# Expert dispatch in a four-stage attention and expert kernel: 64 row scatters into a slot table replaced by 79 row gathers from a token table

## The chip, the cores and the metric

One Trainium2 chip, one core. The metric is the device time of one execution in microseconds (us); the kernel before was run three times. PE is TensorE, ACT is ScalarE, DVE is VectorE, POOL is GpSimd, SP is SyncE.

## What is computed

The input is 16 batches of 128 tokens with 256 channels. Four gated layers follow one another; the change touches only the last, a causal attention followed by a mixture of 16 experts:

```
x2 = rmsnorm(hid, ln2_w).reshape(-1, h)
logits = x2 @ gate_w.T
probs = jax.nn.softmax(logits, axis=-1)
top_w, top_i = jax.lax.top_k(probs, TOPK)                      # TOPK = 4 of E = 16
top_w = top_w / jnp.sum(top_w, axis=-1, keepdims=True)
wfull = jnp.sum(jax.nn.one_hot(top_i, E) * top_w[..., None], axis=1)
gu = jnp.einsum('th,eih->tei', x2, w1)                         # I = 176
act = jax.nn.silu(gu[..., :I]) * gu[..., I:]
routed = jnp.einsum('te,teh->th', wfull, jnp.einsum('tei,ehi->teh', act, w2))
shared = jax.nn.silu(sg) * su @ sh_down_w.T                    # hidden size 352
return hid + (routed + shared).reshape(b, s, h)
```

There are 2048 tokens, so 8192 pairs of token and expert. The kernel sorts them by expert into 79 tiles of 128 slots; a tile belongs to one expert, and slots that are left over in an expert's last tile are empty.

## The kernel before

The last layer ends in two blocks. The first, `sort_and_share` (tiles named e_), normalises the tokens, scores them against the 16 experts, picks four for each, works out the slot of each pair, and computes the shared expert for all tokens. The second, `routed_experts` (tiles named t_), loops over the 79 tiles. A block begins when all engines have ended the one before it.

**sort_and_share.** DVE computes the routing in a chain of small operations, each waiting for its predecessor (`chained`). Its last result is `idx` (L2599), for every token the numbers of its four slots. POOL then issues 64 indirect DMAs (L2342), one for each batch and each of the four choices: each writes 128 rows of 288 floats (the normalised token, 16 expert weights, 16 copies of the token's number) from `rows` to the slots of the DRAM table `slot_rows`, with at most three in flight. The table had been filled with blank rows early in the kernel by one DMA of SP (L787), so that empty slots hold weight zero and a destination in a part of the result that is thrown away. Beside the scatters the shared expert runs in 12 units (4 groups of tokens by 3 tiles of hidden columns): PE `gates_and_values(t)` then `down(t-2)`, ACT `gates(t)` (L2437) then `round_hid(t-1)` (L2443), DVE `hidden(t)` (L2496), `rest_hid(t-1)` (L2501), after each group `add_group` (L2508), and in units 5 to 7 the `tables` that tell the loop which expert each tile has. All four engines work through their lists in order.

**Expert weights.** Each expert's 128x704 weights are loaded into one of 5 buffers (`mw_raw`) and split into a high part by ACT (L2208) and a low part by DVE (L2214). Experts 0 to 4 are split on ACT ahead of the shared expert and on DVE in units 0 to 4; experts 5 to 15 are split once the shared expert is done, because their place in the tile `w_all` holds the shared expert's operands until then.

**routed_experts.** For tile t SP loads 128 slot rows (L2671, six buffers), PE turns them (L2745), ACT and DVE split them into two parts (L2724, L2828), PE multiplies by the gate and value weights (L2764 to L2766), ACT applies silu (L2709), DVE multiplies by the value and the weight (L2822), PE turns the hidden tile (L2773) and multiplies by the second weight (L2783), ACT copies the result to `ysb` (L2714, four buffers), and POOL scatters its 128 rows with an adding indirect DMA into the DRAM tensor `slot_results` (L2700). DVE takes the weight and the destination of each slot out of the slot row with three operations (L2802, L2810, L2815), three tiles ahead; the last of them, `place`, also waits for a scatter some tiles back. POOL issues scatter t only when scatter t-2 has landed. Every 16 tiles PE loads the experts of the next 16 tiles into registers. When all scatters have landed, the two planes of results are loaded and added to x.

Of the kernel before, what the change touches and what calls it, by code (L numbers as in the profile page):

```python
# [7 lines left out]
F32 = mybir.dt.float32  # L8
# [666 lines left out]
def bit_linear_ffn(nc, res, gate_w, val_w, out_w, bias, bias_part, out_b, gate, blank_rows, work):  # L675
# [7 lines left out]
    with ExitStack() as stack:  # L683
# [84 lines left out]
        with nc.Block() as block:  # L768

            @block.sync  # L770
            def _(sp):
# [15 lines left out]
                sp.dma_start(slots.rearrange("(u r) n -> u r n", r=Y_BUFS * P),  # L787
                             fill.unsqueeze(0).broadcast_to([TABLE // Y_BUFS, Y_BUFS * P, ROW])).then_inc(filled, 16)
# [1385 lines left out]
META = 2 * EXPERTS  # L2174
ROW = DIM + META
# [3 lines left out]
EARLY = 5  # L2179
# [9 lines left out]
class ExpertWeights:  # L2189

    def __init__(self, nc, stack, w, w2):
# [6 lines left out]
        self.pick = s.sb("pick", [P, TABLE, EXPERTS], BF16)  # L2198
        self.ld_d = s.sem("ld_d")
# [3 lines left out]
    def load(self, sp, e):  # L2203
        sp.dma_start(self.raw[:, e % RAW_BUFS, :], self.w[e]).then_inc(self.ld_e[e % RAW_BUFS], 16)

# [12 lines left out]
def sort_and_share(nc, x_sb, ident, first, big, ln2, gate_w, gu_w, down_w, consts, gate, slots, filled):  # L2218


    PAD = EXPERTS + 4
    PAIRS = BATCHES // 2
    UNITS_S = GROUPS * SH_TILES
    toks = BATCHES * TOKENS
    spare = [EARLY * 2 * W_COLS]

# [4 lines left out]
    xTh, xTl = (borrow(KT * toks).rearrange("p (k t) -> p k t", k=KT) for _ in range(2))  # L2231
    hid_h, hid_l = (borrow(2 * GT).rearrange("p (a t) -> p a t", a=2) for _ in range(2))
    gu_hf, gu_lf = (borrow(2 * KT * SHARED_HID) for _ in range(2))
    d_hf, d_lf = (borrow(SH_TILES * DIM)[0:SH_ROWS, :] for _ in range(2))
    gu_h, gu_l = (a.rearrange("p (n k c) -> p n k c", n=2, k=KT) for a in (gu_hf, gu_lf))
    d_h, d_l = (a.rearrange("p (j c) -> p j c", j=SH_TILES) for a in (d_hf, d_lf))
    with ExitStack() as stack:
        s = Scope(nc, stack, "e")
        cons = s.sb("cons", [P, P + BATCHES])
        steps = s.sb("steps", [P, EXPERTS * EXPERTS + TABLE])  # L2240
# [3 lines left out]
        raw_gu = s.sb("raw_gu", [P, 2 * KT * SHARED_HID])  # L2244
# [6 lines left out]
        rows = s.sb("rows", [P, BATCHES, ROW])  # L2251
        gw = s.sb("gw", [P, KT, 2, EXPERTS], F32R)
        logits = s.sb("logits", [P, BATCHES, EXPERTS])
# [17 lines left out]
        idx = s.sb("idx", [P, BATCHES, TOPK], mybir.dt.int32)  # L2271
        passed = s.sb("passed", [P, TABLE, EXPERTS + 1], BF16)
        owner = s.sb("owner", [1, TABLE])
        silu = s.sb("silu", [P, 2, GT])
        hid = s.sb("hid", [P, 2, GT])
# [6 lines left out]
        n_ps = l_ps[:, 0, 0, :]  # L2282
        ld_n, ld_g, ld_c, ld_t, ld_s = s.sem("ld_n"), s.sem("ld_g"), s.sem("ld_c"), s.sem("ld_t"), s.sem("ld_s")
# [6 lines left out]
        token_set, c_psum, n_psum = s.sem("token_set"), s.sem("c_psum"), s.sem("n_psum")  # L2290
        idx_ready, meta_ready, sh_hi, sh_lo = s.sem("idx_ready"), s.sem("meta_ready"), s.sem("sh_hi"), s.sem("sh_lo")
# [3 lines left out]
        sent_rows = [s.sem(f"sent_rows{k}") for k in range(IN_FLIGHT)]  # L2295
# [4 lines left out]
        with nc.Block() as block:  # L2300

            @block.sync
            def _(sp):
# [9 lines left out]
                sp.dma_start(first.down[:, :], first.w2).then_inc(first.ld_d, 16)  # L2313
                for n in range(RAW_BUFS, EXPERTS):
                    sp.wait_ge(first.w_lo, n - RAW_BUFS + 1)
                    first.load(sp, n)

            @block.gpsimd
            def _(pool):
# [9 lines left out]
                pool.wait_ge(ld_c, 32)  # L2329
                pool.tensor_copy(rows[:, :, DIM + EXPERTS:ROW],  # L2330
                                 cons[:, P:P + BATCHES].unsqueeze(2).broadcast_to([P, BATCHES, EXPERTS]))\
                    .then_inc(token_set, 1)

                pool.wait_ge(filled, 32)
                pool.wait_ge(token_set, 1)
                pool.wait_ge(idx_ready, 1)
                pool.wait_ge(meta_ready, 1)
                for b in range(BATCHES):
                    for k in range(TOPK):
                        n = TOPK * b + k  # L2340
                        after(pool, sent_rows[n % IN_FLIGHT], 16 * (n // IN_FLIGHT))
                        pool.indirect_dma_start(slots[:, :], bass.IndirectOffsetOnAxis(idx[:, b, k:k + 1], 0),  # L2342
                                                rows[:, b, :], None).then_inc(sent_rows[n % IN_FLIGHT], 16)
                for k in range(IN_FLIGHT):
                    pool.wait_ge(sent_rows[k], 16 * len(range(k, BATCHES * TOPK, IN_FLIGHT)))

            @block.tensor
            def _(pe):
# [8 lines left out]
                def score(m):  # L2357
# [3 lines left out]
                    for b in range(2 * m, 2 * m + 2):  # L2361
                        tok = slice(P * b, P * b + P)
                        for k in range(KT):
                            pe.matmul(l_ps[:, b, :, :], xTh[:, k, tok], gw[:, k, :, :], start=(k == 0), stop=False)
                            mm = pe.matmul(l_ps[:, b, :, :], xTl[:, k, tok], gw[:, k, :, :], start=False,
                                           stop=(k == KT - 1))
# [18 lines left out]

                def gates_and_values(t):
                    (g_, j), p = divmod(t, SH_TILES), t % 2
                    r, c, tok = slice(0, width(j)), slice(SH_ROWS * j, SH_ROWS * j + width(j)), slice(GT * g_, GT * g_ + GT)
                    if t == 0:
                        pe.wait_ge(sh_lo, 2)  # L2390
                    for n, ps, free, done in ((0, g_ps, silu_ready, g_psum), (1, u_ps, hid_ready, u_psum)):
                        after(pe, free, t - 1)
                        for kt in range(KT):
                            h, l = gu_h[:, n, kt, c], gu_l[:, n, kt, c]
                            pe.matmul(ps[p][r, :], h, xTh[:, kt, tok], start=(kt == 0), stop=False)
                            pe.matmul(ps[p][r, :], h, xTl[:, kt, tok], start=False, stop=False)
                            mm = pe.matmul(ps[p][r, :], l, xTh[:, kt, tok], start=False, stop=(kt == KT - 1))
# [25 lines left out]
                for t in range(UNITS_S + 2):  # L2423
                    if t < UNITS_S:
                        gates_and_values(t)
                    if t == 1:
                        tally()
                    if t >= 2:
# [605 lines left out]
```

## Time and profile before

| | us |
|---|---|
| median of 3 runs (lowest to highest) | 1984.11 (1981.86 to 2006.73) |
| the profiled execution | 1989.11 |
| its span in the profile | 1987.3 |

Busy time of the engines over the span: PE 1722.4 us (87%), DVE 1165.0 (59%), ACT 951.5 (48%), POOL 529.5 (27%). `sort_and_share` takes the span's stretch from 1609 to 1756 us, `routed_experts` that from 1756 to the end. An engine's share over the whole span says little here: the layers have different limits, and the change is in the last 380 us. In a timeline each row is an instruction or a run of equal ones: start, duration, engine, line, operation, what it writes and reads, and in brackets how long the engine stood idle before it and what ended that. The duration of an indirect DMA on POOL is the time in which POOL writes its descriptors; the data land later, and the time from issue to landing is in the view of DMA queues.

### The profile page before, as it was taken

What the parts mean: (1) busy time and instruction counts of PE and PEld (TensorE: products, weight loads), DVE (VectorE), ACT (ScalarE), POOL (GpSimd) and SP (SyncE); (2) the same over time, 40 slices, a digit from 0 to 9 for tenths busy, and PEclk for the clock granted to TensorE, in tenths of its full rate; (3) what the DMA queues carried; (4) which work ended last, traced back from release to release, by engine and by line L of the source; (5) the groups of instructions that cost most, each with busy time, mean ns of one, the idle gap of its engine ahead of it and who ended that gap; (6) DMA issues with size and microseconds to landing.
All of it is one profiled execution on the core that took longest, in us unless ns stands there. A gap on an engine that the chain in (4) does not pass through costs nothing. (4 is left out here: it accounts for less than half of the span.)

```text
span 1987.3 us, 34326 instructions
## 1 busy us (share of the span) xinstructions
PE 1722.4 (87%) x11668; PEld 1455.4 (73%) x11668; DVE 1165.0 (59%) x2625; ACT 951.5 (48%) x2452; POOL 529.5 (27%) x527
## 2 busy tenths in 40 slices
PE   7998897697699999999992999999999969259993
PEld 6666664555688888888881788888888867258883
DVE  4688884698655656566546555555555457335553
ACT  2577776486355444545541444444454423225442
POOL 4133321243311111111111111111121114736663
PEclk7699997898899999999996999999999968679997
DMA  4111121265100100100002101001000043447666
GB/s 142 55 34 29 29 70 40 78 252 213 43 13 1 43 12 13 43 1 11 1 1 77 43 1 32 12 12 29 5 12 1 1 117 108 147 101 139 126 115 162
DMA packets 73274, 117.40 MB, mean 59 GB/s; under 512 B 8285, under 2 KB 59021, under 8 KB 71943
## 3 DMA queue, kind: packets, MB, share of 16 engines
q1 hardware_dynamic: 54014, 89.03, 14.4%
q0 software_dynamic: 14448, 19.80, 5.6%
q10 hardware_dynamic: 4648, 6.38, 1.0%
q8 instruction: 103, 1.69, 0.4%
q14 instruction: 61, 0.50, 0.1%
HBM read 86.65 MB, written 44.70 MB: 66 GB/s over the span
## 5 line engine op out<-in xcount | busy, mean ns | idle before, releaser
L1812 ACT ACTIVATE da_prob<-da_prob,da_nb,d_rqs 128x128 f32<-128x128 f32 x256 | 123.3, 483 | 260.2 <-DVE da_nb L2072 260.2
L1812 ACT ACTIVATE hold_wq<-hold_wq,ca_nb,c_rqs 128x128 f32<-128x128 f32 x256 | 123.4, 483 | 235.4 <-DVE ca_nb L2072 235.4
L653 DVE TENSOR_REDUCE a_mx<-a_s 128x2 f32<-128x512 f32 x256 | 167.1, 681 | 60.5 <-PE a_s L541 58.7
L470 ACT ACTIVATE a_prob<-a_s 128x512 f32<-128x512 f32 x256 | 147.4, 600 | 85.7 <-PE a_s L554 85.4
L1874 POOL TENSOR_TENSOR hold_wq<-hold_wq,ca_rsum 128x512 f32<-128x512 f32 x64 | 66.7, 1042 | 428.3 <-DVE ca_rsum L2077 428.3
L1874 POOL TENSOR_TENSOR da_prob<-da_prob,da_rsum 128x512 f32<-128x512 f32 x64 | 66.6, 1041 | 422.9 <-DVE da_rsum L2077 422.9
L2700 POOL DMA_INDIRECT slot_results<-t_ysb,t_dest x79 | 124.3, 1574 | 91.7 <-ACT t_ysb L2714 42.8
L554 PE MATMUL a_s<-a_qs,a_ks 32*128 32x256 f32 x512 | 101.6, 346 | 32.4 <-ACT a_prob L470 32.3
L1884 PE MATMUL da_qk<-d_xTh,da_wqkv_h 128*128 128x512 f32 x256 | 106.7, 417 | 6.4 <-DVE da_wqkv_l L2023 6.4
L541 PE MATMUL a_s<-a_ks,a_qs 32*128 32x256 f32 x512 | 101.0, 351 | 3.1 <-DVE a_mx L653 3.0
L2084 DVE SCALAR_TENSOR_TENSOR ca_oT_l<-ca_oT,ca_bv,ca_oT_h 128x512 fp32r<-128x512 f32 x64 | 48.0, 751 | 93.3 <-ACT ca_oT_h L1826 93.3
L1886 PE MATMUL da_qk<-d_xTh,da_wqkv_l 128*128 128x512 f32 x256 | 101.9, 398 | 0.0
L1885 PE MATMUL da_qk<-d_xTl,da_wqkv_h 128*128 128x512 f32 x256 | 101.6, 397 | 0.0
L554 PEld LDWEIGHTS a_s<-a_qs,a_ks 32*128 32x128 f32 x512 | 61.4, 197 | 48.4 <-ACT a_prob L470 33.3
L2086 DVE TENSOR_TENSOR da_oT_l<-da_oT,da_oT_h 128x512 fp32r<-128x512 f32 x64 | 44.3, 692 | 84.7 <-ACT da_oT_h L1829 84.7
L541 PEld LDWEIGHTS a_s<-a_ks,a_qs 32*128 32x128 f32 x512 | 60.6, 197 | 39.8 <-issue 16.5
L2783 PE MATMUL t_y<-mw_down,t_hTs 88*128 x316 | 83.5, 386 | 3.1 <-ACT t_hTs L2719 3.1
L2342 POOL DMA_INDIRECT slot_rows<-e_rows,e_idx x64 | 67.3, 1051 | 61.5 <-DVE e_idx L2599 37.1
L2745 PE MATMUL t_xT<-ident,t_xg 128*128 128x128 f32 x158 | 30.9, 279 | 56.4 <-DMA t_xg<-slot_rows 56.4
L577 PE MATMUL a_out<-a_prob,a_vT 128*32 128x256 f32 x1024 | 74.6, 412 | 1.2 <-ACT a_prob L470 1.2
L2067 DVE TENSOR_TENSOR da_prob<-da_s,d_causal 128x512 f32<-128x512 f32 x64 | 44.1, 689 | 50.4 <-PE da_s L1913 50.4
L1975 PE MATMUL da_acc<-da_wo_h,da_oT_h 128*128 128x256 f32 x256 | 73.4, 287 | 0.0
(412 smaller groups left out, 5610.2 us busy)
## 6 DMA issues: line engine op xcount, KB each, us to landing
t_xg<-slot_rows SPq DMA_DIRECT2D x79, 144.0 KB, 2.5
mw_raw<-in_d_expert_w SPq DMA_DIRECT2D x16, 352.0 KB, 6.1
slot_results<-in_d_fill SPq DMA_DIRECT2D x1, 4608.0 KB
a_heads<-a_osb SPq DMA_DIRECT2D x128, 32.0 KB
a_wraw<-a_heads SPq DMA_DIRECT2D x32, 128.0 KB, 2.1
mw_down<-in_d_expert_d SPq DMA_DIRECT2D x1, 2816.0 KB
hold_wk<-in_c_wkT SPq DMA_DIRECT2D x1, 2064.0 KB
hold_wq<-in_c_wqT SPq DMA_DIRECT2D x1, 2064.0 KB, 9.0
```

The costliest lines, as they stand in the source:

```text
L470: act.activation(prob[:, w % PR, :, :], s2[w % 2][:, :, :], ACT.Exp, scale=1.0 / A_ROOT)\
L541: mm = pe.matmul(s1[use % S1_BANKS][:, t, :], qs[rows, b % A_BUFS, j, P * t:P * t + P], ks[rows, b % A_BUFS, j, :], start=True, stop=True)
L554: mm = pe.matmul(s2[w % 2][:, t, :], ks[rows, b % A_BUFS, j, P * t:P * t + P], qs[rows, b % A_BUFS, j, :], start=True, stop=True)
L577: mm = pe.matmul(out[A_ROWS * r:A_ROWS * r + A_ROWS, j % 2, :], vT[:, b % A_BUFS, t, A_TILES * r + j, :], prob[:, (U * b + A_SLOTS * j + v ...
L653: dve.tensor_reduce(mx[:, b % 2, :, h], s1[s1_use(b, u) % S1_BANKS][:, :, :], AX.X, ALU.max)\
L1812: ins = act.activation(prob[:, p, b, :], prob[:, p, b, :], ACT.Exp, bias=nb[:, p, b:b + 1], scale=rqs[:, r:r + 1], accum_out=sums[:, p, b: ...
L1874: pool.tensor_tensor(prob[:, k % 2, :, :], prob[:, k % 2, :, :], rsum[:, k % 2, :].unsqueeze(2).broadcast_to([P, GB, TOKENS]), ALU.mult)\
L1884: pe.matmul(out, ah, bh, start=start, stop=False)
L1885: pe.matmul(out, ah, bl, start=False, stop=False)
L1886: return pe.matmul(out, al, bh, start=False, stop=stop)
L2700: pool.indirect_dma_start(results[:, :], bass.IndirectOffsetOnAxis(dest[:, d:d + 1], 0), ysb[:, t % Y_BUFS, :], None, compute_op=ALU.add)\
L2783: mm = pe.matmul(y_ps[t % 2][:, 0:DIM], hT[:, t % 2, k, :], first.down[:, ds(at_d[t] + DIM * k, DIM)], start=(k == 0), stop=(k == 1))
```

## The change

- **No slot table.** The rows of tokens are written once to a DRAM table of 1 + 2048 rows of 272 floats (token and 16 weights), by one DMA of SP behind `meta_ready`. Row 0 is blank. The fill of the slot table becomes a fill of that one row. The token number and POOL's copy of it (L2330) go.
- **Which token sits in which slot** is now worked out on chip. DVE divides the slot number into tile and lane. For each of the 16 batches (`locate`) DVE builds a one-hot of the lane (128x512) and one of the tile (128x320), ACT scales the latter by the token's label (`name`), and PE multiplies the two in four matmuls (`find`). The bits of the sum give each slot's token number, 0 for an empty slot (`identify`). Four batches are handled in each of the units 0 to 3 (PE one unit later), and `identify` stands in unit 4.
- **Gathers.** POOL fetches each tile's 128 rows by an indirect DMA: 28 in the first block after `identify` (three in flight), 8 at the start of the second, and 43 in the loop, spread evenly behind the scatters of tiles 0 to 69. There are 44 tile buffers instead of 6, in space of the rows, a loose area and the raw weights. SP's 79 loads go.
- **In the loop** DVE's three operations for weight and destination become one multiply-and-sum; the destinations of all tiles are computed once, in `identify`.
- **Expert weights.** Experts 5 to 8 are split in units 6 to 11, 9 to 11 once PE's last gate and value product is done, and 12 to 15 after the last `down`.

```diff
-ROW = DIM + META
+ROW = DIM + EXPERTS
+X_OWN, X_LOOSE = BATCHES, 16
+X_EARLY, X_AHEAD, X_BUFS = 28, 36, 44
+X_SEMS = 8
-EARLY = 5
+EARLY, SHARED, BEFORE = 5, 9, 12
...
+    def gather(self, pool, slots, t, behind):
+        if t >= behind:
+            self.fetched(pool, t - behind)
+        pool.indirect_dma_start(self.tile(t), None, slots[:, :],
+                                bass.IndirectOffsetOnAxis(self.ids[:, t:t + 1], 0)).then_inc(self.x_in[t % X_SEMS], 16)
...
+                sp.wait_ge(meta_ready, 1)
+                sp.wait_ge(xn_ready, BATCHES)
+                sp.dma_start(slots[1:1 + BATCHES * TOKENS, :].rearrange("(b p) c -> p b c", p=P), rows[:, :, :])\
+                    .then_inc(rows_stored, 16)
...
-                for b in range(BATCHES):
-                    for k in range(TOPK):
-                        n = TOPK * b + k
-                        after(pool, sent_rows[n % IN_FLIGHT], 16 * (n // IN_FLIGHT))
-                        pool.indirect_dma_start(slots[:, :], bass.IndirectOffsetOnAxis(idx[:, b, k:k + 1], 0),
-                                                rows[:, b, :], None).then_inc(sent_rows[n % IN_FLIGHT], 16)
-                for k in range(IN_FLIGHT):
-                    pool.wait_ge(sent_rows[k], 16 * len(range(k, BATCHES * TOPK, IN_FLIGHT)))
+                pool.wait_ge(ids_ready, 1)
+                for n in range(X_EARLY):
+                    first.gather(pool, slots, n, IN_FLIGHT)
...
+                def find(b):
+                    pe.wait_ge(lane_ready, b + 1)
+                    pe.wait_ge(named_ready, b + 1)
+                    for k in range(TOPK):
+                        mm = pe.matmul(f_ps, in_lane[:, b % DEEP, k, :], named[:, b % DEEP, k, :],
...
+        SPLIT_HI = {6: 5, 7: 6, 9: 7, 10: 8}
+        SPLIT_LO = {4: (0, 1), 5: (2, 3), 6: (4,), 7: (5,), 8: (6,), 10: (7,), 11: (8,)}
...
                 for t in range(UNITS_S):
                     gates(t)
+                    if t < GROUPS:
+                        name(GB * t)
+                        name(GB * t + 1)
                     if t >= 1:
                         round_hid(t - 1)
+                    if t < GROUPS:
+                        name(GB * t + 2)
+                        name(GB * t + 3)
...
+                def locate(b):
+                    after(dve, found_psum, b - DEEP + 1)
+                    dve.tensor_tensor(in_lane[:, b % DEEP, :, :], lane_of[:, b, :].unsqueeze(2).broadcast_to([P, TOPK, P]),
+                                      lanes.unsqueeze(1).broadcast_to([P, TOPK, P]), ALU.is_equal).then_inc(lane_ready, 1)
+                    after(dve, named_ready, b - 1)
+                    dve.tensor_tensor(in_tile[b % 2], tile_of[:, b, :].unsqueeze(2).broadcast_to([P, TOPK, TABLE]),
+                                      times.unsqueeze(1).broadcast_to([P, TOPK, TABLE]), ALU.is_equal).then_inc(tile_ready, 1)
...
                 for t in range(UNITS_S):
                     hidden(t)
+                    if t < GROUPS:
+                        locate(GB * t)
+                        locate(GB * t + 1)
                     if t >= 1:
                         rest_hid(t - 1)
+                    if t < GROUPS:
+                        locate(GB * t + 2)
+                        locate(GB * t + 3)
+                    if t == GROUPS:
+                        identify()
...
+        def rows_by(t):
+            return min(NT, X_AHEAD + (t + 1) * (NT - X_AHEAD) // (NT - X_SEMS - 1))
...
+                for t in range(X_EARLY, X_AHEAD):
+                    first.gather(pool, slots, t, X_SEMS)
                 for t in range(NT):
                     pool.wait_ge(y_copied, t + 1)
-                    pool.wait_ge(dest_ready, t + 1)
                     if t >= PLANES:
                         pool.wait_ge(sent[(t - PLANES) % Y_BUFS], 16 * ((t - PLANES) // Y_BUFS + 1))
...
+                    for n in range(rows_by(t - 1), rows_by(t)):
+                        after(pool, xT_psum, n - X_BUFS + 1)
+                        after(pool, picked, n - X_BUFS + 1)
+                        first.gather(pool, slots, n, X_SEMS)
```

## Rows read from the trace of the kernel before

**Rows 1.** Busy time by stretch: us, instructions in brackets, granted clock, DMA share, GB/s.

```profile
1656.00:1702.00 46.00, 45.71 (x258) 39.14 (x258) 26.37 (x38) 12.53 (x23) 34.66 (x31) 0.96 0.41 137
1702.00:1756.00 54.00, 0.00 (x0) 0.00 (x0) 10.55 (x12) 8.18 (x11) 32.63 (x34) 0.52 0.37 133
1758.00:1966.00 208.00, 188.24 (x1106) 170.00 (x1106) 98.56 (x399) 98.54 (x316) 124.33 (x79) 0.95 0.66 116
```

**Rows 2.** Timeline across both blocks: first and last row scatter, first loads and transposes.

```profile
1656.53 1.51 POOL L2342 DMA_INDIRECT slot_rows<-e_rows,e_idx  x1 [37.10 <-DVE e_idx L2599]
...
1747.29 0.96 POOL L2342 DMA_INDIRECT slot_rows<-e_rows,e_idx  x1 [0.30 <-issue]
1756.11 3.70 SPq L2671 DMA_DIRECT2D t_xg<-slot_rows  x8
...
1758.27 1.19 PE L2745 MATMUL t_xT<-ident,t_xg 128*128 128x128 f32 x4 [56.38 <-DMA t_xg<-slot_rows]
```

**Rows 3.** Timeline of DVE beside the shared expert.

```profile
1655.33 0.19 DVE L2599 TENSOR_SCALAR e_idx<-e_first 128x64 int32<-128x64 f32 x1
...
1697.35 0.69 DVE L2496 TENSOR_TENSOR e_hid<-e_silu,e_turned 116x512 f32<-116x512 f32 x1 [1.61 <-PE e_turned L2397]
1697.95 0.68 DVE L2501 TENSOR_TENSOR w_all<-e_hid,w_all 118x512 fp32r<-118x512 f32 x1
...
1701.93 1.22 DVE L2508 TENSOR_TENSOR x_sb<-x_sb,e_acc 128x1024 f32<-128x1024 f32 x1 [1.78 <-PE e_acc L2414]
```

**Rows 4.** Groups by line and shape from 1600 to 1760 us: busy us, mean ns.

```profile
L2437 ACT ACTIVATE e_silu<-e_turned 118x512 f32<-118x512 f32 x8 | 4.7, 597 | 19.5 <-PE e_turned L2397 19.5
...
L2457 ACT ACTIVATE e_e<-e_sh 128x256 f32<-128x256 f32 x1 | 0.4, 416 | 4.1 <-DVE e_sh L2558 4.1
...
L2593 DVE TENSOR_TENSOR e_sh<-e_c,e_base 128x256 f32<-128x256 f32 x1 | 0.4, 424 | 0.0
```

**Rows 5.** Timeline of POOL: a scatter beside DVE's `rest_hid`, and the 36th scatter.

```profile
1698.09 1.39 POOL L2342 DMA_INDIRECT slot_rows<-e_rows,e_idx  x1 [0.30 <-issue]
...
1708.29 0.96 POOL L2342 DMA_INDIRECT slot_rows<-e_rows,e_idx  x1 [0.30 <-issue]
```

**Rows 6.** The expert weights' tile: durations min/median/max in ns, and landing in us.

```profile
L2208 ACT ACTIVATE w_all<-mw_raw x16: 772/777/792, 1645.2 to 1715.3; 128x704 fp32r<-128x704 f32 x16
L2214 DVE TENSOR_TENSOR w_all<-mw_raw,w_all x16: 883/886/935, 1656.0 to 1716.1; 128x704 fp32r<-128x704 f32 x16
...
DMA to landing us min/median/max: 2.9/6.1/21.9
```

**Rows 7.** Timeline of POOL in the loop: the first, two neighbouring, and the last adding scatter.

```profile
1768.75 1.61 POOL L2700 DMA_INDIRECT slot_results<-t_ysb,t_dest  x1 [20.50 <-ACT t_ysb L2714]
...
1778.15 1.55 POOL L2700 DMA_INDIRECT slot_results<-t_ysb,t_dest  x1 [0.30 <-issue]
...
1962.77 1.55 POOL L2700 DMA_INDIRECT slot_results<-t_ysb,t_dest  x1 [0.72 <-DMA slot_results<-t_ysb,t_dest]
```

**Rows 8.** The chain that ended last, in the loop: the same step of neighbouring tiles.

```profile
1774.00 0.87 PE t_y L2783 x4
...
1776.27 0.86 PE t_y L2783 x4
```

**Rows 9.** Waits in the loop: us in total, times, longest.

```profile
DVE t_dest L2815 <- DMA slot_results<-t_ysb,t_dest: 24.4, 23, 3.7
...
POOL slot_results L2700 <- DMA slot_results<-t_ysb,t_dest: 18.2, 16, 3.1
```

**Rows 10.** DMA queue of POOL (packets, MB, share) and landing, from 1640 to 1757 us.

```profile
q0 software_dynamic: 3072, 9.44, 20.8%
...
slot_rows<-e_rows,e_idx POOLq DMA_INDIRECT x64, 2.4
```

**Rows 11.** The same view from 1760 to 1960 us.

```profile
q0 software_dynamic: 10944, 9.97, 41.8%
...
slot_results<-t_ysb,t_dest POOLq DMA_INDIRECT x77, 3.9
```

More of the change, by code:

```diff
@@ L2198, in __init__ @@
         self.pick = s.sb("pick", [P, TABLE, EXPERTS], BF16)
+        self.rows = s.sb("rows", [P, X_OWN, ROW])
+        self.loose = s.sb("loose", [P, X_LOOSE * ROW])
+        self.ids = s.sb("ids", [P, TABLE], mybir.dt.int32)
+        self.dest = s.sb("dest", [P, TABLE], mybir.dt.int32)
+        self.x_in = [s.sem(f"x_in{k}") for k in range(X_SEMS)]
         self.ld_d = s.sem("ld_d")
@@ L2221, in sort_and_share @@
     PAD = EXPERTS + 4
+    DEEP = 8
+    LABEL = 127 * P
     PAIRS = BATCHES // 2
@@ L2443, in round_hid, with name @@
                     act.activation(hid_h[r, t % 2, :], hid[r, t % 2, :], ACT.Copy).then_inc(hid_hi, 1)
+                def name(b):
+                    act.wait_ge(tile_ready, b + 1)
+                    after(act, found_psum, b - DEEP + 1)
+                    act.activation(named[:, b % DEEP, :, :], in_tile[b % 2], ACT.Copy, scale=cons[:, P + b:P + b + 1])\
+                        .then_inc(named_ready, 1)
                 act.wait_ge(ld_g, 16)
@@ L2605, in _ @@
                         add_group(t // SH_TILES - 1)
-                    if t < EARLY:
-                        first.split_lo(dve, big, t)
-                    if EARLY <= t < EARLY + 3:
-                        tables(t - EARLY)
+                    for n in SPLIT_LO.get(t, ()):
+                        first.split_lo(dve, big, n)
+                    if GROUPS + 3 <= t < GROUPS + 6:
+                        tables(t - GROUPS - 3)
                 rest_hid(UNITS_S - 1)
+                for n in range(SHARED, BEFORE):
+                    first.split_lo(dve, big, n)
@@ L2611, in _ @@
                 add_group(GROUPS - 1)
-                dve.wait_ge(acc_psum, UNITS_S)
-                for n in range(EARLY, EXPERTS):
+                for n in range(BEFORE, EXPERTS):
                     first.split_lo(dve, big, n)
@@ L2619, in routed_experts @@
 def routed_experts(nc, x_sb, ident, first, big, before, slots, results, out):
-    X_BUFS, D_BUFS = 6, 8
+    D_BUFS = 8
     with ExitStack() as stack:
         s = Scope(nc, stack, "t")
-        xg = s.sb("xg", [P, X_BUFS, ROW])
+        xg = first.tile
         xh = s.sb("xh", [P, 2, KT, P], F32R)
@@ L2639, in routed_experts @@
         y_ps = [s.ps(f"y{k}", [P, 512]) for k in range(2)]
-        x_in = [s.sem(f"x_in{k}") for k in range(X_BUFS)]
         sent = [s.sem(f"sent{k}") for k in range(Y_BUFS)]
```

208 lines of the change are left out of this document (118 added, 90 removed).

## The prediction

> **What bounds the kernel now.** I read the page's 40 slices first, then the busy time by stretch [rows 1]. While the shared expert runs (1656 to 1702 us), PE is busy for 45.7 of 46 us. From 1702 to 1756 it does nothing. From 1758 to 1966 it is busy for 188 of 208 us. The hole is what a reader should see first: DVE and ACT fill 10.6 and 8.2 us of it with expert weights, POOL 32.6 us with row scatters. The timeline [rows 2] says what ends it: the last of 64 scatters is issued at 1747.29, lands some 2.4 us later [rows 10], and the loop's first load leaves at 1756.11, so 6.4 us go by between landing and the next block. PE turns its first tile at 1758.27.
>
> In the loop two clocks run side by side. Neighbouring tiles are 2.27 us apart on PE's chain [rows 8]. POOL needs 1.55 us for an adding scatter and 0.30 us before the next instruction [rows 7], 1.85 us per tile, so it has slack. But 78 steps from the first scatter to the last take 1962.77 - 1768.75 = 194.0 us, 2.49 each. Part of the difference to 2.27 is waits for landed scatters, 24.4 us on DVE and 18.2 us on POOL [rows 9], which overlap one another.
>
> **The change, part by part.** The sum has four terms, made against the profiled run's own time.
>
> *1. When the gathers can start.* Before, POOL starts when `idx` is done, at 1655.5 [rows 3]. Now the slot number passes four chained operations of about 0.2 us in place of one: 1656.1. Then come the 16 `locate`. The trace has no one-hot of this size. DVE's 128x256 operation takes 0.42 us and its 128x512 ones 0.68 with starts 0.60 apart [rows 3, 4], so I take 0.60 for 512 columns and 0.40 for 320, 1.0 us per batch. DVE also has to wait for ACT twice in a unit: `rest_hid` and the next `hidden` stand behind a `name` that waits for the last `locate`. `name`, 320 columns, lies between 0.42 us (256 columns) and 0.60 us (512) [rows 4]; I take 0.45. With the silu or rounding of 0.6 us and the hand-overs each wait is 1.15 us. Unit 0: 0.6 + 4.0 + 1.15 = 5.8. Units 1 to 3: 0.6 + 0.6 + 4.0 + 2 x 1.15 = 7.5 each. Unit 4 begins at 1656.1 + 5.8 + 22.5 = 1684.4; `hidden`, `rest_hid` and three small operations later the ids stand at 1686.3. PE's 64 bf16 matmuls of 80 columns and the rows' one store (issued after the weights are ready, before `idx`) lie beside this. If ACT never holds DVE, the ids come some 8 us sooner; if each one-hot costs as the 0.69 us rows, 6 us later.
>
> *2. Until the block ends.* The trace has scatters, no gathers. A row scatter costs 0.96 us when DVE is idle [rows 2] and 1.39 when it meets `rest_hid` [rows 5]; an adding one costs 1.55 [rows 7]. A gather copies rows as the plain scatter does and adds nothing. The adding queue moved 10944 packets for 77 scatters, the plain one 3072 for 64 [rows 11, 10]: it is adding that takes one packet per row. So I take 0.96 and keep 1.55 as the dear end. Beside the shared expert and the weight splits 36 scatters left from 1656.53 to 1708.29 [rows 2, 5]: 35 steps of 1.48 us, waits and gaps included. 27 x 1.48 + 1.26 = 41.2: the last gather is issued at 1727.5. The other road to the block's end is DVE's. Before, `hidden` went from 1655.5 to 1697.35 in eleven units of 3.8 us [rows 3], and unit 4 began near 1670.7; now it begins 13.7 us later, and units 4 and 5 carry four weight splits, so the shared expert ends near 1717 in place of 1703. Experts 9 to 11 are split on the way; the loads of 14 and 15 leave only when 9 and 10 are split, land in about 6 us, and take 0.78 + 0.89 us [rows 6]: 1725. POOL's road is the later by a little. With the same 6.4 us to the next block and no load ahead of PE, the first tile is turned at 1733.9. **Saved: 24.4 us.**
>
> POOL writes descriptors while DVE compares and subtracts. Stretching comes from operations with two inputs in SBUF, as `rest_hid` is; the page "SBUF — State Buffer" of the Trainium skill, section "SBUF: two separate sides", says that such an operation and a GpSimd one can lock each other out for a whole instruction. By that rule the 28 gathers run at 1.26 to 1.7 us and those in the loop, where DVE's long operations read PSUM, at 1.26; the row of 1.39 agrees.
>
> *3. The loop.* POOL now issues 8 gathers first (8 x 1.26 = 10.1 us), about as long as the first result takes to come (1768.75 - 1758.27 = 10.5 us before). From there 78 steps of 1.85 us and 43 gathers of 1.26 us: 144.3 + 54.2 = 198.5. Over tiles 0 to 69 this is 2.62 us per tile, more than PE's 2.27 and more than the 2.49 of before: **POOL becomes the bound**, and its backlog, up to the four `ysb` buffers, hides PE's own stalls, the register loads among them. In the last nine tiles no gather stands between; the backlog drains at half a landing (3.9 / 2 = 1.95) and then at PE's 2.27, 2.5 us in all over 1.85. First turn to last scatter: 10.2 + 198.5 + 2.5 = 211.2 us, against 1962.77 - 1758.27 = 204.5. **Lost: 6.7 us.** DVE's three small operations becoming one and SP's loads going cost and bring nothing: neither engine is on the path. The waits of [rows 9] go, but into POOL's own time.
>
> *4. Elsewhere.* The fill of the slot table ran beside the second layer, and I take nothing for it. The end, from the last scatter on, is unchanged.
>
> Sum: -24.4 + 6.7 = -17.7 us. The profiled run, 1989.1, would be 1971.4. It lies 5.0 above the median of three, so the forecast for the median is 1984.1 - 17.7 = 1966.4, **1966 us**. Its own range is 1956 to 1976.
>
> **Rivals.**
> - *The loop stays PE's.* If a gather takes POOL well under 0.96 us, say 0.5, a tile costs it 1.85 + 0.61 x 0.8 = 2.34 us, and the end comes at PE's pace with a few register loads, 2.40: 10.2 + 78 x 2.40 = 197.4, 7 us less than before: 1966 - 14 = 1952. The first block gains 2 us more, until the weight splits hold its end. With the ids 8 us sooner as well it could reach 1942. Against it: no indirect DMA in the trace is under 0.95.
> - *A gather costs as an adding scatter*, the case on the other side. At 1.55 us, 0.59 more: 28 x 0.59 = 16.5 in the first block, 51 x 0.59 = 30.1 in the loop, 1966 + 47 = 2013. It turns from gain to loss where 79 gathers cost 17.7 us more, that is at 1.18 us each; being stretched to 1.39 by DVE in the loop would be enough (1966 + 51 x 0.43 = 1988). For it: both the stretched row and the adding ones exist. Against: in the loop the adding scatters lie at 1.55 with hardly a stretch.
> - *Scatters land late behind gathers.* Before, the loop's loads were SP's; now both kinds are POOL's. Scatter t+2 waits for t, and with a gather between they leave 4.96 us apart, so landing may grow from 3.9 to 4.96 for nothing. By the share of their queue [rows 10] a row scatter takes 0.208 x 117 / 64 = 0.4 us of all engines: 4.3, still free. If a full gather's landing came on top, 3.9 + 2.4 = 6.3 us for two tiles, 70 tiles would take 220 in place of 184: 2002. The page "DMA: Bandwidth & Descriptors" of the Trainium skill, section "SWDGE vs HWDGE vs iDMA", says that software-made transfers have one queue and that an engine goes round between it and the hardware-made ones; by that the gathers, unlike SP's loads, do stand ahead of the scatters, and this trace, which has never two kinds in that queue, can't show it.
> - *The routing detour is cheaper or dearer than worked out*: the ends of term 1, 1958 and 1972.
>
> **How the numbers follow.** The forecast has 0.55 with both ends of the detour in it, PE's loop 0.17, the dear gather 0.16 (half of it stretched, near 1988, half at 2013), late landing 0.08, something unforeseen 0.04. The range that leaves out no more than 2 in 10 is **1947 to 1990**. 2% is 40 us, about what a measurement of this kernel can tell from no change: under 1944 only the best of PE's loop reaches, **0.11**; over 2024 only a dear gather with late landing, **0.05**; between, **0.84**.
>
> **What would show it.** The hole without PE should shrink from 56 us to about 15, between some 1717 and 1734. The ids should come near 1686, with DVE idle before `hidden` and `rest_hid` for ACT in units 1 to 3. A gather in POOL's timeline should read 0.96, and 1.3 to 1.4 beside the shared expert. In the loop POOL should have no idle time but 0.30 us gaps, PE should wait for ACT's copy, and ACT for landed scatters; the steps should be 2.6 us apart. If POOL idles in the loop, the bound is elsewhere; if gathers read over 1.2, there is no gain; if the block's last event is a weight split well after the last gather, term 2 is wrong.

## The result: half a per cent faster, and where it went

| | before | after |
|---|---|---|
| median of 20 runs each, us | 1991.4 (1981.9 to 2006.7) | 1980.6 (1976.8 to 1999.1) |
| ratio | | 0.9953 (95%: 0.9933 to 0.9973) |
| profiled run, us / span | 1989.1 / 1987.3 | 1987.3 / 1985.5 |
| block's start (POOL's `e_half` memset) | 1609.05 | 1614.66 |
| first turn, from the block's start | 149.2 | 126.8 |
| first turn to last adding scatter | 204.5 | 218.5 |
| from there to the end of the span | 24.5 | 25.6 |

By the ratio the kernel is 9.3 us faster, with an interval of 5.4 to 13.3 (the two medians lie 10.8 apart). More runs of before moved its median from 1984.1 to 1991.4, so the forecast of 1966 is best read as its change, -17.7 us: right in direction, nearly twice too large.

The two spans differ by 1.8 us only. The code ahead of this block is all but the same in both kernels (one large fill is gone from it), and yet the block starts 5.6 us later in the profile after; in the other profiles shown here it starts between 1606.4 and 1620.1 us. So I compare times counted from the block's start. Counted so, the two profiles differ by 378.2 - 370.8 = 7.4 us, and the table splits them: 22.5 saved, 14.0 lost in the loop, 1.1 lost at the end.

First the busy time by stretch of the kernel after, the view of [rows 1]: the gathers beside the shared expert, the hole, and the loop.

```profile
1693.52:1726.00 32.48, 30.12 (x180) 26.01 (x180) 26.94 (x36) 13.26 (x22) 23.91 (x21) 1.00 0.61 186
1726.00:1741.41 15.41, 0.00 (x0) 0.03 (x1) 4.04 (x5) 2.00 (x3) 7.79 (x8) 0.52 0.38 120
...
1752.04:1943.00 190.96, 176.48 (x1020) 157.20 (x1019) 69.22 (x293) 88.92 (x291) 155.62 (x114) 0.96 0.58 90
```

PE stands still for 16.6 us between the blocks (the row of PE below) where it stood for 56.4 [rows 2]. These 39.8 us did not all become gain, because the shared expert beside the routing now ends later: DVE's last addition into `x_sb` starts 110.8 us from the block's start, and was at 92.9 [rows 3]. In the loop POOL, the last of the five engine columns, is busy for 155.6 of 191 us; nearly all the rest is 0.30 us gaps.

The handover in the timeline, the view of [rows 2] (start, duration, engine, line):

```profile
1726.66 1.63 POOL L2228 DMA_INDIRECT mw_loose<-token_rows,mw_ids  x1 [0.30 <-issue]
1729.47 0.94 POOL L2228 DMA_INDIRECT mw_loose<-token_rows,mw_ids  x1 [1.18 <-DMA mw_loose<-token_rows,mw_ids]
...
1736.39 0.94 POOL L2228 DMA_INDIRECT mw_loose<-token_rows,mw_ids  x1 [0.30 <-issue]
...
1741.41 1.08 PE L2849 MATMUL t_xT<-ident,mw_rows 128*128 128x128 f32 x4 [16.61 <-PEq L42]
...
1742.02 0.95 POOL L2228 DMA_INDIRECT mw_loose<-token_rows,mw_ids  x1 [4.68 <-POOLq L42]
```

The 28th gather ends at 1737.33 and the next block begins; DVE's last weight split had ended at 1732.4, so POOL's list holds the block's end, by 5 us. One gather is stretched to 1.63 us beside two of DVE's weight splits, one waits 1.18 us for an earlier one to land.

POOL in the loop, answering to [rows 7]:

```profile
1752.04 1.64 POOL L2801 DMA_INDIRECT slot_results<-t_ysb,mw_dest  x1 [0.30 <-issue]
1753.98 1.58 POOL L2801 DMA_INDIRECT slot_results<-t_ysb,mw_dest  x1 [0.30 <-issue]
1755.87 1.02 POOL L2228 DMA_INDIRECT mw_raw<-token_rows,mw_ids  x1 [0.30 <-DMA slot_results<-t_ysb,mw_dest]
...
1959.88 1.57 POOL L2801 DMA_INDIRECT slot_results<-t_ysb,mw_dest  x1 [0.82 <-DMA slot_results<-t_ysb,mw_dest]
```

Nothing but 0.30 us lies between POOL's instructions: a scatter occupies it for 1.88 us, a gather for 1.32. Who waits now, the view of [rows 9], from 1742 to 1962 us:

```profile
DVE t_xl L2920 <- ACT t_xh L2828: 95.5, 71, 2.4
ACT t_ysb L2818 <- DMA slot_results<-t_ysb,mw_dest: 41.3, 27, 2.1
```

ACT waits 41.3 us for scattered results, and DVE waits for ACT: the four `ysb` buffers are full, because POOL is behind.

POOL's whole loop can be added up from its rows, from the first scatter's start to the last one's. This sum, in us, is the key to the case:

| | before | after |
|---|---|---|
| 78 scatters | 122.7 | 122.5 |
| 43 gathers | - | 44.1 |
| 0.30 us gaps | 23.4 | 36.3 |
| waits beyond the gaps | 47.7 | 4.5 |
| first to last scatter | 194.0 | 207.8 |

(Waits of less than 0.1 us beyond a gap are left out, so the rows add up to 193.8 and 207.4.) 57.0 us of gathers and their gaps went into 47.7 us of idle time, of which 43.2 could be filled. What didn't fit is the loss.

### The profile page after: what moved, and what is told of

The parts are those of the page before. It is cut to its first block and busy times, and to the rows that moved or that the text cites. A ratio compares the mean times of both kernels' runs of the same rounds, so it can differ in the third digit from the quotient of the medians.

```text
span 1985.5 us, 34204 instructions
## 1 busy us (share of the span) xinstructions
PE 1740.2 (88%) x11723; PEld 1463.1 (74%) x11732; DVE 1159.5 (58%) x2587; ACT 958.7 (48%) x2468; POOL 545.8 (27%) x541
## 5 line engine op out<-in xcount | busy, mean ns | idle before, releaser
L2801 POOL DMA_INDIRECT slot_results<-t_ysb,mw_dest x79 | 123.9, 1569 | 28.6 <-issue 19.5
L2920 DVE TENSOR_TENSOR t_xl<-t_xT,t_xh 128x256 fp32r<-128x256 f32 x79 | 33.5, 425 | 95.6 <-ACT t_xh L2828 95.5
L2066 DVE TENSOR_TENSOR da_prob<-da_s,d_causal 128x512 f32<-128x512 f32 x64 | 44.1, 690 | 50.5 <-PE da_s L1912 50.5
L1974 PE MATMUL ca_acc<-ca_wo_h,ca_oT_h 128*128 128x256 f32 x256 | 73.0, 285 | 0.1
```

Source lines behind the costliest of these rows:

```text
L1974: pe.matmul(acc[:, b, :], ah, bh, start=(h == 0 and b % 2 == 0), stop=False, skip_group_check=True)
L2801: pool.indirect_dma_start(results[:, :], bass.IndirectOffsetOnAxis(first.dest[:, t:t + 1], 0), ysb[:, t % Y_BUFS, :], None, compute_op=ALU ...
```

## Experiments

My theory after the result: in the loop POOL's time per tile is the bound, and in the block before it the 28 gathers behind the ids are; the gain is one minus the other. The rivals were that other engines, landings, or the later start of the second half of the shared expert hold either of them. Times "from the block's start" begin at the same memset as in the table above. "The loop" is the stretch from the first adding scatter's start to the last one's. Where one total time is given, the kernel ran once; the argument then rests on its profile.

**Taking the loop's gathers away.** The tiles take the first 36 tiles' rows again, and 43 gathers are left out.

```diff
...
-            return min(NT, X_AHEAD + (t + 1) * (NT - X_AHEAD) // (NT - X_SEMS - 1))
+            return X_AHEAD
```

> Leaves out the 43 gathers in the loop: tiles 36 to 78 read the rows of tiles 0 to 42 again. Theory (POOL bounds the loop): POOL needs 1.87 us a tile, PE 2.27, so the steps from first to last scatter fall from 207.8 us to PE's pace of 2.3 to 2.4 a tile, 180 to 187 us: 21 to 28 us less. Rival (landing of scatters or PE's own stalls bound the loop): 3 us less at most.

Measured: 187.1 us from the first to the last scatter in place of 207.8; the run took 1959.2 us. POOL's groups and waits from 1744 us on:

```profile
L2802 POOL DMA_INDIRECT slot_results<-t_ysb,mw_dest x79 | 123.8, 1567 | 65.2 <-ACT t_ysb L2819 29.2 <-DMA slot_results<-t_ysb,mw_dest 26.2 <-issue 9.9
```

POOL's scatters cost the same 1567 ns, and POOL is idle for 65.2 us again, gaps included, for ACT's copy and for landings. The 57 us of gathers and gaps cost the loop 20.7. That is also more than the 13.8 by which the loop of the kernel after is longer than that of the kernel before: without the gathers the loop is faster than the old one, whose 194.0 held waits of its own (below).

**Taking the adding away.** The scatters overwrite, and so the sum of a token's results is left out.

```diff
-    ysb[:, t % Y_BUFS, :], None, compute_op=ALU.add).then_inc(sent[t % Y_BUFS], 16)
+    ysb[:, t % Y_BUFS, :], None).then_inc(sent[t % Y_BUFS], 16)
```

> Leaves out the adding in the loop's scatters: results overwrite one another. Theory (POOL bounds the loop, and adding is what makes its scatter dear): a scatter takes 0.95 in place of 1.57 us, POOL 1.25 + 0.61 x 1.32 = 2.06 us a tile, under PE's 2.27; first to last scatter 180 to 187 us in place of 207.8. Rival (a scatter costs POOL the same without adding): no change. Rival (landing bounds the loop): less than 5 us.

Measured: 184.4 us of loop, 1965.8 us in all. Its group in the loop:

```profile
L2801 POOL DMA_INDIRECT slot_results<-t_ysb,mw_dest x79 | 77.2, 977 | 50.0 <-ACT t_ysb L2818 32.7 <-DMA slot_results<-t_ysb,mw_dest 9.2 <-issue 7.7
```

A scatter costs 977 ns where an adding one costs 1569; with all gathers in place, POOL has slack again. So it is the sum on POOL that counts, not the gathers as such: take 57 us of one kind away or 46 of the other, and the loop falls to 2.36 to 2.40 us per tile, near the 2.27 of PE's chain [rows 8]. In the run without gathers 19.9 us of POOL's waits are still for landed scatters.

**Gathering nothing ahead in the loop.** `X_AHEAD` 28 in place of 36: the 8 gathers that POOL issues before the first result comes are spread over the loop's tiles.

```diff
-X_EARLY, X_AHEAD, X_BUFS = 28, 36, 44
+X_EARLY, X_AHEAD, X_BUFS = 28, 28, 44
```

> Computes the same; no gathers ahead of the loop's first scatter, 51 instead of 43 spread over tiles 0 to 69. Theory (POOL has no slack in the loop): POOL idles for the 10 us until the first result and issues the eight gathers later, so the last scatter comes 10 us later. Rival (the loop has slack at PE's side that absorbs them): within 2 us.

Measured: 218.1 us of loop (after: 207.8), with 51 gathers in it, 51.9 us of them, and 38.7 of gaps; POOL waits 4.4 us beyond them. 8 gathers at 1.32 us are 10.6, and the loop is 10.3 longer. First turn to last scatter grows by 9.0; in the first 10 us of the loop, in which POOL has no result to send, the 8 gathers cost only the 1.2 us by which they delay the first scatter (10.6 us after the first turn, and 9.4 without them). The whole kernel took 1993.6 us.

**The order beside the shared expert.** ACT takes the next unit's silu and the rounding of `hid` between two pairs of `name`, and DVE does all four `locate` of a unit behind `rest_hid`. Nothing is left out or added. The order in short, not the code's own lines:

```diff
 ACT, per unit of the first four
-    gates(t); name 0, 1; round_hid(t - 1); name 2, 3
+    name 0, 1; gates(t + 1); round_hid(t); name 2, 3
 DVE
-    hidden(t); locate 0, 1; rest_hid(t - 1); locate 2, 3
+    hidden(t); rest_hid(t - 1); locate 0, 1, 2, 3
```

> Computes the same; in units 0 to 3 ACT applies silu and rounding ahead of the last two names, and DVE does hidden and rest_hid first and then its four locates, so neither waits for the other. Theory (POOL's list runs without a gap from the ids to the last scatter, so whatever brings the ids forward brings the end forward): DVE loses 7 waits of 1.1 us, the ids come 8 us sooner after the block's start (78.9 us in the changed kernel), and the last scatter too; 8 us less than the changed kernel, a ratio to the kernel before of 0.991. Rival (the block's end is held by the weight splits or the shared expert, or the loop by PE): the ids come sooner, the end moves by less than 3 us, ratio 0.994 to 0.995.

Measured: the first gather leaves 71.7 us after the block's start (after: 78.9), PE's first turn comes at 117.0 (126.8), the last scatter at 335.9 (345.2). The median is 1979.2 us, the ratio to before 0.9930 (0.9903 to 0.9956); on the chip of the last group, 0.9911 (0.9883 to 0.9940). DVE's seven waits for ACT are gone, each of which looked like these two of the kernel after (timeline of DVE):

```profile
1667.68 0.69 DVE L2566 TENSOR_TENSOR mw_loose<-mw_loose,e_turned 118x512 f32<-118x512 f32 x1 [1.11 <-ACT mw_loose L2489]
...
1671.53 0.69 DVE L2571 TENSOR_TENSOR w_all<-mw_loose,w_all 118x512 fp32r<-118x512 f32 x1 [1.15 <-ACT w_all L2495]
```

7 x 1.13 = 7.9 us of waits, and the first gather leaves 7.2 us sooner. The last scatter comes 9.3 sooner, but part of that is scatter: the first block is the same in the kernel after and in the three runs above, and its first turn came at 126.8, 125.2, 124.5 and 123.8 us. Against their mean of 125.1 the reordered kernel's 117.0 is 8.1 sooner, with the same loop behind it. So the gain goes through, because POOL's chain behind the ids sets the block's end. The whole times show less of it: 1979.2 us is 1.4 under the median of the kernel after, which ran in another group, and the intervals of the two ratios (0.9903 to 0.9956, and 0.9933 to 0.9973) overlap.

**More gathers in flight.** The reordered kernel with 8 gathers under way in the first block, not 3.

```diff
-IN_FLIGHT = 3
+IN_FLIGHT = 8
```

> The reordered kernel with up to 8 gathers in flight in the first block, in place of 3. If the stalls in which POOL waits for a landed gather there (0.70, 1.08 us and others) are what keeps 28 gathers at 40.4 us against 27 x 1.26 + 0.95 = 35, then they should fall by some 3 us to 37 or 38, and PE's first turn should come 2 to 3 us sooner. If the stretch of the instruction beside DVE's two-input operations (1.2 to 1.6 us in place of 0.95) is the cause, they stay near 40 and only the rows with a DMA wait vanish into them.

Measured: from the first gather's start to the last one's end 37.6 us in place of 41.3 (from start to start 36.6 and 40.4). POOL's groups there:

```profile
L2228 POOL DMA_INDIRECT mw_rows<-token_rows,mw_ids x16 | 18.0, 1125 | 66.4 <-DVE mw_ids L2695 61.9 <-issue 4.6
L2228 POOL DMA_INDIRECT mw_loose<-token_rows,mw_ids x12 | 11.3, 944 | 3.7 <-issue 3.7
```

No wait for a landing is left. With 3 in flight these waits took 2.9 us (41.3 less 30.4 of instructions and 8.1 of gaps); the rest of the 3.8 is a stretch that fell by 1.1, as DVE worked less beside it. What stays above 0.945 us is the stretch of the 16 rows of the first group, 2.9 us. The first turn did not come sooner (124.8 us from the block's start, against 117.0; 1983.0 us in all): on the chip on which this group of kernels ran, PE, ACT and DVE stood still for up to 13.9 us beside the shared expert, for no releaser that the profile shows, so that POOL was no longer last. What the deeper queue is worth at the turn stays open.

**The kernel before with half its row scatters.** Half of the slot rows aren't written, the rest is unchanged.

```diff
-                for b in range(BATCHES):
+                for b in range(BATCHES // 2):
                     for k in range(TOPK):
```

> The kernel before with only 32 of its 64 row scatters, so that half of the slot rows aren't written: it leaves out half of the dispatch. If POOL's scatters alone held the block's end open, as I read the hole without PE, the 33rd to 64th (32 x 1.26 = 40 us) fall away until the weight splits, the last of which ended near 1717 to 1725, hold it: the first turn comes 30 to 35 us sooner than 1758.3 relative to the block's start, and the loop keeps its 194 us. If something else, the weights' loads say, held it beside the scatters, less than 20 us are gained.

Measured (timeline): the first turn at 116.9 us from the block's start, 32.3 sooner than before; the loop takes 194.1 us, as before.

```profile
1726.52 1.33 PE L2745 MATMUL t_xT<-ident,t_xg 128*128 128x128 f32 x4 [15.73 <-DMA t_xg<-slot_rows]
```

So POOL's scatters alone held the old hole open; with half of them the weight splits end it, 32 us sooner. It would have been some 6 us more but for this run's standstills (ACT stood for 15.0 us beside the shared expert with no releaser in the profile): its last split ended 113.8 us from the block's start, that of the kernel before at 108.0. So 32 to 38 us were there to be won from POOL, and this change won 22.5. The whole run took 1958.4 us.

**The kernel before with 16 destination buffers.** DVE's `place` no longer waits for the scatter of eight tiles ago.

```diff
-    X_BUFS, D_BUFS = 6, 8
+    X_BUFS, D_BUFS = 6, 16
```

> The kernel before with 16 destination buffers in place of 8, so that DVE's place(t) no longer waits for the scatter of tile t-8 (24.4 us of DVE's waits there). If that wait is what makes the old loop's step 2.49 us and not the 2.27 of PE, the first to the last scatter takes about 78 x 2.30 = 180 us in place of 194.0. If the landing is held by POOL's own wait for scatter t-2, or PE's stalls set the step, the wait moves to POOL or ACT and the loop stays at 192 to 194.

Measured: 190.5 us of loop in place of 194.0. POOL waits 46.0 us beyond its gaps, against 47.7. What ends these waits moved from DVE's `dest` (16.1 to 9.2 us) and landings (13.4 to 4.4) to ACT's copy (15.4 to 29.6). The old loop's 2.49 us per tile were thus only in small part that wait; the rest are other stops, whose shares weren't separated. The whole run, 1995.8 us, can't be compared: ACT stood still for 38.6 us ahead of the weight splits with no releaser, and the first turn came at 157.6 us and not at 149.2.

**A plane for each rank, no adding.** Since the adding cost 0.6 us on the engine that bounds the loop, this version of the reordered kernel has four result planes, one for each of a token's four ranks. PE finds the ids in four groups of 80 columns, `dest` is id + 2048 x rank, the scatters overwrite, the planes need no zeros, and the end loads and adds 16 times in place of 8. Nothing of the computation is left out.

```diff
-PLANES = 2
+PLANES = 4
...
-                        mm = pe.matmul(f_ps, in_lane[:, b % DEEP, k, :], named[:, b % DEEP, k, :],
+                        mm = pe.matmul(f_ps[:, k, :], in_lane[:, b % DEEP, k, :], named[:, b % DEEP, k, :],
...
-                    if t >= PLANES:
-                        pool.wait_ge(sent[(t - PLANES) % Y_BUFS], 16 * ((t - PLANES) // Y_BUFS + 1))
-                                            ysb[:, t % Y_BUFS, :], None, compute_op=ALU.add)...
+                                            ysb[:, t % Y_BUFS, :], None)...
```

> The reordered kernel (1979.2 us, ratio 0.993) with one result plane for each of a token's four ranks in place of two planes with adding: 77 plain scatters, no wait of scatter t for scatter t-2, no zero fill of the planes, twice as many plane loads (16 in place of 8) and additions at the end. My theory, from the run that left the adding out (loop 184.4 us against 207.8): the loop's first to last scatter is 184 to 187 us, some 22 less than 208.1, and each scatter reads about 0.97 in place of 1.57 us. The end grows: 8 loads took some 15 us after the last scatter, and 8 more of them should add 10 to 14 us. Net -8 to -12 us: 1967 to 1971 us, ratio about 0.988. The rival: the plane loads' 4 MB more cost as much as the loop gives (25 us), or ids wait longer for the wider operations; then the kernel stays at 1979.

Measured: 2002.9 us, ratio 1.0021 (0.9984 to 1.0058). The loop took 217.3 us, in which POOL stood for 60.5 beyond its gaps. Waits in it, from 1750 to 1955 us:

```profile
DVE t_xl L2932 <- issue: 20.5, 19, 2.8
...
ACT t_ysb L2829 <- remote: 16.3, 8, 2.6
```

"remote" and "issue" are times in which the profile shows nothing that the engine waited for. All four kernels of this group ran on one chip, and all show such standstills beside the shared expert. In the loop only this one was visibly slowed: the two versions of the kernel before took 190.5 and 194.1 us there, the one with eight gathers in flight 208.1. The kernel before ran at 1998.4 us there against 1992.5 on the chip of the first group. So it was run again, beside one with the wait for the scatter of two tiles ago put back, and beside the reordered kernel.

```diff
+                    if t >= 2:
+                        pool.wait_ge(sent[(t - 2) % Y_BUFS], 16 * ((t - 2) // Y_BUFS + 1))
                     pool.indirect_dma_start(results[:, :], ...
```

> The kernel with a plane for each rank and plain scatters, with one wait put back: scatter t waits until scatter t-2 has landed, as in the kernel that left the adding out. That kernel's loop took 184.4 us with POOL waiting 27.6 us beyond its gaps; without the wait, and with four planes, it took 217.3 us, in which POOL waited 60.5 us, mostly for ACT's copy, and PE and ACT stood for 1 to 4 us several times with no releaser in the profile. If the many scatters and gathers in flight hold up the rest, the wait put back brings the loop to 184 to 190 us and the kernel to 1965 to 1972 us. If the stalls come from elsewhere (the chip that it ran on, the four planes' addresses), the loop stays near 217 and the kernel near 2000.

> The kernel with a plane for each rank once more, unchanged, beside the other two. If its slow loop (217.3 us) belongs to the kernel, it is 1.0 to 1.02 of before again, with stalls of PE and ACT in the loop; if it was that one chip's, it comes to 0.985 to 0.99 with a loop of 184 to 187 us.

> The reordered kernel once more, as the yardstick for the other two on the same chip: 0.993 of before, a loop of 208 us with POOL never idle but for its gaps. If this chip disturbs PE's issue, POOL's bound hides it and the loop stays 208.

| on one chip | median, us | ratio to before | loop, us | after the last scatter, us |
|---|---|---|---|---|
| reordered | 1973.8 | 0.9911 (0.9883 to 0.9940) | 207.8 | 25.6 |
| planes by rank | 1968.5 | 0.9893 (0.9847 to 0.9938) | 183.7 | 40.2 |
| the same with the wait | 1962.9 | 0.9866 (0.9831 to 0.9901) | 183.6 | 40.0 |

No "remote" wait is left in any of the three. The slow loop is thus no property of the kernel alone: the same code took 217.3 us in one group and 183.7 in the other. Nor is it one of the chip alone, as the other three loops of that group show. What the two did together, or whether the hour and not the chip made the difference, stays open. Here the wait put back changes nothing in the loop. The busy time by stretch of the last of them, loop and end:

```profile
1735.16:1919.73 184.57, 175.62 (x1067) 160.25 (x1066) 73.35 (x301) 94.92 (x306) 121.07 (x122) 1.00 0.32 99
1919.73:1958.70 38.97, 0.00 (x0) 0.00 (x0) 19.61 (x16) 0.00 (x0) 0.00 (x0) 0.50 0.82 272
```

PE is now busy for 175.6 of 184.6 us at a granted clock of 1.00, the DMA share falls from 0.58 to 0.32. The 24 us gained in the loop cost 14.4 at the end, where 16 planes must be read before the last addition. This is the fastest median of all versions that compute everything, 1.3% under the kernel before; it isn't clear of the version without the wait, as the intervals of the two overlap. Over the reordered kernel its four runs are clear (1960.6 to 1969.4 us against 1969.7 to 1979.3), those without the wait are not.

## Why the prediction was wrong: the loss in the loop was too small by half

The forecast change was -17.7 us; the two profiles give -7.4 and the 20 runs each -9.3. The step that failed is term 3, the loop: 6.7 us of loss were forecast and 14.0 measured. The other differences between forecast and profile are 1.9 us in the first block and 1.1 at the end.

*Term 1, the ids.* Right in its mechanism and nearly in size. The one-hots start 0.60 and 0.40 us apart, the waits in units 1 to 3 are 1.11 and 1.15 us where 1.15 was written; `name` takes 0.56 us and not 0.45, and stands in each of those waits. The first gather leaves at 78.9 us from the block's start, the ids were forecast at 77.2. Of the 1.7 us, the step from DVE's last cast to POOL's start is 0.95, which I had left out though the old scatters had a like one behind `e_idx` [rows 2, 3]. That the ids would come some 8 us sooner without ACT's waits is borne out by the reordered kernel, 7.2.

```profile
1692.37 0.20 DVE L2693 CAST mw_ids<-e_sel 128x80 int32<-128x80 f32 x1
...
1693.52 1.24 POOL L2228 DMA_INDIRECT mw_rows<-token_rows,mw_ids  x1 [68.82 <-DVE mw_ids L2693]
```

*Term 2, the block's end.* 28 gathers take 43.8 us; 41.2 was forecast, from the step of 1.48 us of the old scatters. They divide into 31.7 us of instructions, 8.1 of gaps and 4.0 of landings. The handover from the last gather's end to the first turn takes 4.1 us and not 6.4. The 6.4 ran from the old scatters' landing to the first load and already left the load out; why it is longer than 4.1 no run tells. Together the first turn is 1.9 us later than forecast: 22.5 saved, not 24.4. That difference is no failure of the term: in the four profiles with this same first block the turn came at 123.8 to 126.8 us, so that 22.4 to 25.4 were saved, 24.1 at their mean. With 24.1 the sum of the measured terms is -9.0, next to the -9.3 of the runs. That POOL holds the end and the weight splits come just before it was right.

The handover also depends on which engine is last. In eight profiles a gather of POOL ended the block, and the first turn came 3.95 to 4.10 us later. In the two in which a weight split of DVE ended it (eight gathers in flight, and the slow run with four planes), the turn came 1.03 and 1.02 us later. So POOL being last seems to cost some 3 us more than its last gather; but both of these runs were on the chip with the standstills, and no run was made to test it.

The 28 gathers are 5.2 us longer than at the 0.945 us that they take in the hole, 1.13 us on average, or 1.43 with the gap. The page "SBUF — State Buffer" of the Trainium skill, section "SBUF: two separate sides", was cited for 1.26 to 1.7 us each, gap included. The trace agrees in part: all 12 gathers that took 1.07 to 2.04 us had an operation of DVE with two inputs in SBUF beside them. But five more had one beside them for 0.6 to 0.9 us and still took 0.95, so that meeting such an operation isn't enough.

*Term 3, the loop.* Here the forecast failed: 14.0 us lost, not 6.7. It is the same in the other runs of this loop: first turn to last scatter took 218.5, 218.9 and 218.4 us in the kernel after and the two undisturbed profiles of the reordered one. The mechanism was right, POOL is the bound, with no idle time but its gaps and 4.5 us. Of the signs that were named, one did not show: it is DVE and not PE that waits for ACT (95.5 us; PE waits 9.6). The size was off because the result is a small difference of large sums. Its parts, measured against forecast:

| us | forecast | measured |
|---|---|---|
| first turn to first scatter | 10.2 | 10.6 |
| 78 scatters with gaps | 144.3 (1.85 each) | 145.9 (1.87) |
| 43 gathers with gaps | 54.2 (1.26 each) | 57.0 (1.32) |
| remaining waits | 2.5 | 4.5 |
| sum | 211.2 | 218.0 (first to last event: 218.5) |

Each part but the last is 1 to 5% too low and the whole 3.5%, yet all of the 7.3 us fall on a loss of 6.7. A gather takes 0.95 us in a row of gathers and 1.02 between scatters; the scatter behind it takes 1.58, the next 1.55. I had priced every instruction by its undisturbed row. The last nine scatters have three waits of 1.0 to 1.6 us for ACT's copy between them, and one of 0.8 for a landing. That is 3.8 of the 4.5 us, where 2.5 were forecast.

*Term 4.* The end behind the last scatter is 1.1 us longer, not unchanged; no run tells why. It may be scatter: the kernel before and its two versions show 24.5, 24.7 and 25.5 us. That the fill brings nothing held, as far as the scatter of the block's start allows to say.

*The rivals.* The loop staying PE's is excluded (POOL idle 4.5 us). A gather as dear as an adding scatter is excluded: all 79 take 1.06 us on average, against the 1.18 at which the prediction saw the gain turn into a loss. Late landing is excluded as well: a scatter behind gathers lands in 3.8 us where it was 3.9 [rows 11], the gathers in 2.9 to 3.5 (in the first block, beside the loads of expert weights, in 3.8 to 3.9). The page "DMA: Bandwidth & Descriptors" of the Trainium skill, section "SWDGE vs HWDGE vs iDMA", says that software-made transfers have one queue. The trace agrees: from 1745 to 1945 us it counts the packets of 72 scatters and 49 gathers, 12639, under one software queue. The price of sharing it is zero here.

```profile
slot_results<-t_ysb,mw_dest POOLq DMA_INDIRECT x79, 3.8
mw_loose<-token_rows,mw_ids POOLq DMA_INDIRECT x20, 3.5
mw_rows<-token_rows,mw_ids POOLq DMA_INDIRECT x16, 2.9
```

*The level.* The forecast for the median took the median of three runs, 1984.1. Twenty gave 1991.4. A forecast of a few us should carry that uncertainty too; it is as large as the error in the loop. Of the 14 us by which the kernel after is slower than the forecast of 1966, 7 are this level.

## What to carry to other kernels

When work moves to an engine that had slack, write its whole account first, instruction by instruction with gaps and waits, before and after: the slack that can be filled (43 of 47.7 us here) and the work put in (57.0) are both large, and the result is their difference, so prices that are 1 to 5% too low double the loss. Of two kinds of instruction on the engine that bounds, look at the dearer one, whoever put it there: the adding, not the new gathers, had 0.6 us per tile to give. And an engine waiting for another in the middle of a fixed order (1.1 us, seven times) is worth a look whenever its chain sets a block's end: the reordering cost nothing, and in the profiles it won almost all of it.

## What I had not expected of the hardware

A gather costs POOL 0.94 to 0.95 us behind another gather and 1.02 (the median) when adding scatters are between. Between plain scatters it takes 0.98 to 0.99, but there a few are stretched to 1.5, so that the mean is 1.02 there too. An adding scatter costs 1.57, a plain one to the same rows 0.98.

Where POOL's gathers end a block, POOL's work in the next one starts 4.6 to 4.7 us later, although nothing is loaded in between, and PE's 4.0 to 4.1 us later. Where DVE ended it, PE's started after 1.0.

On one chip a kernel lost 34 us in its loop to standstills of ACT and DVE that the profile puts down to nothing (217.3 against 183.7 us with the same code elsewhere), while a loop bound by POOL took 208.1 us there, and two loops of the kernel before, in which POOL idles for 46 to 49 us, took 190.5 and 194.1. What stands still, and why only in that loop, is not known; a kernel that looks slow in one group is worth a second run in another.
